# Router logits of an attention and mixture-of-experts kernel: from x and the attention output as nine more columns of Wo, instead of from the normed rows

## What is computed

```python
x1 = x + attention(layernorm(x), ctx)            # 16 heads of 16; ends with  out @ Wo + bo
xn2 = layernorm(x1)
logits = xn2 @ Wr                                # 8 experts
w, experts = top_2(softmax(logits)), softmax of the two
y = x1 + sum over the two experts of  w * (silu(xn2 @ gate) * (xn2 @ up)) @ down
```

## Time and profile before

| | before |
|---|---|
| median of 3 runs | 1244.41 us |
| the profiled execution, its own time | 1243.54 us |
| its span, first to last instruction | 1241.8 us |
| busy: PE, DVE, ACT, POOL | 97%, 52%, 45%, 34% |
| granted TensorE clock, mean | 0.996 |
| moved by DMA | 112.43 MB |

### The profile page before, as it was taken

How to read it: one execution, slowest core, us unless ns; L and a number is a source line. 1 busy time by engine, 2 the same in 40 slices (tenths; PEclk the granted TensorE clock), 3 DMA queues, 4 the chain that set the end, 5 groups by cost and what they waited for, 6 DMA issues and landing times.

```text
span 1241.8 us, 30499 instructions
## 1 busy us (share of the span) xinstructions
PE 1209.8 (97%) x11102; PEld 989.2 (80%) x11103; DVE 645.0 (52%) x1744; ACT 562.3 (45%) x926; POOL 425.4 (34%) x356
## 2 busy tenths in 40 slices
PE   7999999999999999899999999999999999999996
PEld 5777777777667766688888888888888888888995
DVE  3778888888788878834462222222222222222332
ACT  4566666666666666535422222222222222222542
POOL 4112333333333333253454422222222222222322
PEclk9999999999999999999999999999999999999998
DMA  5444455455455432434444433333333333333432
GB/s 148 135 118 126 148 155 151 149 159 154 151 154 153 123 117 88 101 86 62 75 78 80 70 51 52 51 51 51 51 51 51 51 51 51 52 51 41 54 51 31
DMA packets 171585, 112.43 MB, mean 91 GB/s; under 512 B 103344, under 2 KB 158640, under 8 KB 171472
## 3 DMA queue, kind: packets, MB, share of 16 engines
q1 hardware_dynamic: 143984, 72.75, 24.0%
q0 software_dynamic: 26400, 37.09, 17.3%
q10 hardware_dynamic: 1088, 1.05, 0.2%
HBM read 48.59 MB, written 45.46 MB: 76 GB/s over the span
## 4 chain that ended last, share of the span: by engine, by line
PE 93%; DVE 3%; DMA 2%; issue 1%; ACT 1%; SPq 0%; POOLq 0%; DVEq 0%
PE banks L545 73%; PE banks L574 5%; PE banks L588 5%; PE banks L599 5%; PE banks L580 1%; PE banks L551 1%; PE banks L615 1%; DMA heads<-qT 1%; PE banks L623 1%; DVE row_max L1088 1%; DMA out<-x_sb,token 1%; DMA ctxT_sb<-in_ctx 1%; DVE q_less L1095 0%; DVE att_rows L1101 0%; SPq L293 0%
## 5 line engine op out<-in xcount | busy, mean ns | idle before, releaser
L494 POOL DMA_INDIRECT out<-x_sb,token x135 | 210.6, 1560 | 418.9 <-DVE x_sb L1402 373.5
L919 ACT ACTIVATE qT<-banks 128x1024 f32<-128x1024 f32 (+1 forms) x75 | 70.4, 939 | 462.8 <-PE banks L545 441.5
L1396 DVE TENSOR_TENSOR heads<-qT,banks 128x1024 f32<-128x1024 f32 (+1 forms) x75 | 83.6, 1114 | 346.8 <-PE banks L545 339.0
L545 PE MATMUL banks<-down_sb,heads 128*128 x1080 | 245.5, 379 | 0.9 <-DVE heads L1396 0.9
L545 PE MATMUL banks<-xnT,kT 128*128 128x256 f32 (+1 forms) x1216 | 243.0, 357 | 0.0
L545 PE MATMUL banks<-xnT,probs 128*128 128x256 f32 (+1 forms) x1184 | 238.7, 359 | 0.0
L545 PEld LDWEIGHTS banks<-xnT,kT 128*128 128x128 f32 x1216 | 211.9, 190 | 25.5 <-issue 0.2
L545 PEld LDWEIGHTS banks<-xnT,probs 128*128 128x128 f32 x1184 | 208.3, 190 | 25.2 <-issue 0.2
L545 PEld LDWEIGHTS banks<-down_sb,heads 128*128 128x128 f32 x1080 | 204.0, 190 | 28.2 <-issue 1.1
L443 POOL DMA_INDIRECT sorted_x<-xn,slots_now x128 | 125.5, 980 | 275.2 <-PE banks L574 133.1
L1088 DVE TENSOR_REDUCE row_max<-banks 128x16 f32<-128x2048 f32 x64 | 146.6, 2291 | 51.0 <-PE banks L574 50.8
(11 more groups left out here) (172 smaller groups left out, 1272.0 us busy)
## 6 DMA issues: line engine op xcount, KB each, us to landing
xn<-sorted_x SPq DMA_DIRECT2D x240, 64.0 KB
x_sb<-in_x SPq DMA_DIRECT2D x16, 512.0 KB, 3.9
ctxT_sb<-in_ctx SPq DMA_DIRECT2D x16, 512.0 KB
heads<-kT SPq DMA_DIRECT2D x128, 64.0 KB
heads<-qT SPq DMA_DIRECT2D x128, 64.0 KB
out<-x SPq DMA_DIRECT2D x16, 512.0 KB
gate_sb<-_L_ffn_kernel_gating_EDF SPq DMA_DIRECT2D x8, 512.0 KB
up_sb<-in_L_ffn_kernel_up_EDF SPq DMA_DIRECT2D x8, 512.0 KB
```

The costliest lines, as they stand in the source:

```text
L494: pool.indirect_dma_start(out=out[:, :], out_offset=bass.IndirectOffsetOnAxis(ap=token[:, v, h:h + 1], axis=0), in_=ys[:, 2 * u + h, :], i ...
L545: last = nc.tensor.matmul(dst, lhsT, rhs, start=(i == 0), stop=(i == len(pairs) - 1))
L919: nc.scalar.activation(gatedT[:, 0:w * F], all_banks[:, 1024 * place:1024 * place + w * F], ACT.Silu).then_inc(s_silu, 1)
L1396: nc.vector.tensor_tensor(fusedT[:, u, 0:w * F], gatedT[:, 0:w * F], gate_up[:, 1024:1024 + w * F], ALU.mult).then_inc(s_fuse, 1)
```

## The change

The logits of a normed row are rstd * (x1 Wr - mean * colsum(Wr)). And x1 Wr = x Wr + attn (Wo Wr) + a constant. So:

- `wo_sb` gets 9 more columns: Wo Wr (8) and minus their sum, so that the sum over a row of 265 is still the sum over 256. `project` and `add_residual` work on 265 columns (`WIDE`); x1 and x_bo are as wide.
- The host hands over x transposed and Wo transposed as well. SP loads x's second layout once per group (512 KB) in b=1. `route_logits(g)` takes x Wr of the group itself from it in b=0, `swap_logits(g)` follows in b=1, and DVE adds the constants and writes them to x_bo's 9 columns (`keep_x_logits`).
- `x1_swapped` and `copy_x1T` are gone (8 transposes and 2 copies a group).
- DVE keeps the raw logits of a complete group in b=1 (`keep_raw`, two operations with both operands in SBUF), and multiplies by rstd one group later in `route_shift` (one operation more).
- At the start: Wo Wr and the constants are made on TensorE within sequences 0 and 1; four small DVE operations ahead of them.
- After stage A only `places` and the count are left on TensorE between the units.

```diff
+WIDE = D + EXPERTS + 1
...
+            def load_xT(g):
+                wait(sp, s_logitT, g)
+                sp.dma_start(xT_sb[:], xT[:, bass.ds(g * GROUP * TOK, GROUP * TOK)].rearrange("(c p) t -> p c t", p=P)).then_inc(s_xT, 16)
...
             spread_queries(1)
+            sp.dma_start(woT_sb, woT.rearrange("(c p) n -> p c n", p=P)).then_inc(s_woT, 16)
+            load_xT(0)
...
                     if b == 1 and g > 0:
                         store_x1(g - 1)
+                    if b == 1 and g + 1 < GROUPS:
+                        load_xT(g + 1)
...
-                product(bank[:, 0:D], [(attnT[:, c * P:(c + 1) * P], wo_sb[:, c, :]) for c in range(DC)]).then_inc(s_proj, 1)
-
-            def x1_swapped(g, c, bank):
...
+                product(bank[:, 0:WIDE], [(attnT[:, c * P:(c + 1) * P], wo_sb[:, c, :]) for c in range(DC)]).then_inc(s_proj, 1)
...
             def route_logits(g, bank):
 
-                wait(pe, s_n2Tc, g * 2 + 2)
+                wait(pe, s_xT, g * 16 + 16)
...
                         wait(pe, s_less, i * 2 + 2)
-                        if b == 1 and prev2:
-                            wait(pe, s_route, (g - 2) * ROUTE_STEPS + SHIFTED)
+                        if b == 1:
+                            wait(pe, s_x_logits, g + 1)
                         norm_swapped(g + 1, b, other_bank(i, 3))
-                    if b >= 2 and prev:
-                        wait(pe, s_less, i * 2 + 2)
-                        x1_swapped(g - 1, b - 2, other_bank(i, 3))
-                    if b == 0 and prev2:
+                    if i == 0:
+                        wo_through_router(other_bank(i, 0))
+                    if b == 0 and core:
                         wait(pe, s_turn, i)
...
+            def keep_x_logits(g, u, bank):
+                wait(dve, s_logit, g + 1)
+                nc.vector.tensor_tensor(x_bo[:, u, :, D:WIDE], bank[:, 0:GROUP * 32].rearrange("p (s e) -> p s e", e=32)[:, :, 0:EXPERTS + 1],
+                                        bias_logits.unsqueeze(1).broadcast_to([P, GROUP, EXPERTS + 1]), ALU.add).then_inc(s_x_logits, 1)
+
+            def keep_raw(g):
+                wait(dve, s_x1, g * GROUP + GROUP)
+                wait(dve, s_route, (g - 1) * ROUTE_STEPS + 1)
+                nc.vector.tensor_tensor(raw_mean[:], over_group(router_sums), over_experts(x1_sum[:]), ALU.mult).then_inc(s_raw, 1)
+                wait(dve, s_raw, g * 2 + 1)
+                nc.vector.scalar_tensor_tensor(raw[:], raw_mean[:], -1.0 / D, x1[:, :, D:D + EXPERTS], ALU.mult,
+                                               ALU.add).then_inc(s_raw, 1)
+
+            def route_shift(g):
                 steps = Steps(dve, s_route, g * ROUTE_STEPS)
...
+                steps.then(nc.vector.tensor_tensor(logits[:], raw[:], over_experts(rstd2[:]), ALU.mult))
+                steps.then(nc.vector.reduce_max(best[:], logits[:], AX.X))
+                steps.done(nc.vector.tensor_tensor(logits[:], logits[:], over_experts(best[:]), ALU.subtract))
```

More of the change, by code:

```diff
@@ L134, in moe_attention @@
         logitsT = sb("logitsT", [P, TOK])
+        raw, raw_mean = sb("raw", GE), sb("raw_mean", GE)
+        router_sum = sb("router_sum", [P, DC])
+        bo_col = sb("bo_col", [P, DC])
+        router_consts = sb("router_consts", [P, 2, EXPERTS + 1])
+        bias_logits, router_sums = router_consts[:, 0], router_consts[:, 1, 0:EXPERTS]
         chosen = sb("chosen", GE, bf16)
@@ L314, in _ @@
             sp.wait_ge(s_zero, 1)
[L315 to L318, removed]
+            sp.dma_start(wr_sb[:, :, 0:EXPERTS], router.rearrange("(c p) e -> p c e", p=P)).then_inc(s_wr, 16)
+            sp.dma_start(bo_col[:], bo.rearrange("(c p) -> p c", p=P), allow_slow_non_contiguous=True).then_inc(s_bo_col, 16)
             sp.wait_ge(s_rows, 2)
@@ L654, in stage_a @@
                     wait(pe, s_turn, i - 1)
-                    if b == 1 and prev2:
-                        wait(pe, s_logitTc, g - 1)
-                    if b == 2 and prev2:
-                        wait(pe, s_route, (g - 2) * ROUTE_STEPS + SHIFTED)
+                    if b == 1 and core:
+                        wait(pe, s_logitTc, g + 1)
+                    if i == 1:
+                        pe.wait_ge(s_wo_wide, 1)
+                    if b == 2 and core:
+                        wait(pe, s_x_logits, g + 1)
                     if b == 3 and prev2:
@@ L700, in stage_a @@
                         wait(pe, s_less, i * 2 + 2)
+                        wait(pe, s_x_logits, 1)
                         norm_swapped(1, 1, other_bank(i, 3))
@@ L741, in _ @@
             pe.wait_ge(s_bv_rep, 1)
-            product(work[:, 0, 0:D], [(bv_rep[:, c, :], wo_sb[:, c, :]) for c in range(DC)]).then_inc(s_bvo, 1)
+            product(work[:, 0, 0:D], [(bv_rep[:, c, :], wo_sb[:, c, 0:D]) for c in range(DC)]).then_inc(s_bvo, 1)
             pe.wait_ge(s_piece_c, 2)
@@ L1334, in stage_a @@
                         first_stats(g + 2, (2, 3))
+                    if b == 1 and core:
+                        wait(dve, s_logit, g + 1)
+                    if i == 1:
+                        dve.wait_ge(s_consts_r, 1)
+                        nc.vector.tensor_copy(router_consts[:], other_bank(i, 3)[:, 2 * P:2 * P + 32].rearrange(
+                            "p (k e) -> p k e", e=16)[:, :, 0:EXPERTS + 1]).then_inc(s_wo_wide, 1)
+                    take_max_off(i, other_bank(i, 3))
+                    if i == 0:
+                        dve.wait_ge(s_wo_wr, 1)
+                        nc.vector.tensor_copy(wo_sb[:, :, D:WIDE], other_bank(i, 0)[:, 0:32].rearrange(
+                            "p (c e) -> p c e", e=16)[:, :, 0:EXPERTS + 1]).then_inc(s_wo_wide, 1)
+                    if i == 1:
+                        dve.wait_ge(s_wo_wide, 2)
+                    if b == 1 and core:
+                        keep_x_logits(g, u, other_bank(i, 3)[:, P:2 * P])
                     if b == 1 and prev2:
-                        wait(dve, s_logit, g - 1)
-                    take_max_off(i, other_bank(i, 3))
-                    if b == 1 and prev2:
-                        route_shift(g - 2, other_bank(i, 3)[:, P:2 * P])
+                        route_shift(g - 2)
                     if b == 2 and prev2:
@@ L1365, in stage_a @@
                         route_first(g - 2)
+                    if b == 1 and prev:
+                        keep_raw(g - 1)
                     if b == 3 and g == EARLY_GROUPS + 2:
@@ L1416, in behind_tile @@
                 if t == 3:
+                    route_shift(GROUPS - 2)
+                    keep_raw(GROUPS - 1)
                     second_eps(GROUPS - 1)
-                if t == 5:
-                    route_shift(GROUPS - 2, att)
                 if t == 6:
@@ L1431, in behind_tile @@
                 if t == 12:
-                    route_shift(GROUPS - 1, att)
+                    route_shift(GROUPS - 1)
                     route_first(GROUPS - 1)
```

125 lines of the change are left out of this document (57 added, 68 removed).

## The result

| | before | after |
|---|---|---|
| median | 1244.49 us (4 runs, 1242.09 to 1245.66) | 1279.94 us (4 runs, 1274.21 to 1282.84) |
| ratio, 95% interval | | 1.0282 (1.0242 to 1.0321) |
| the profiled execution, its own time | 1243.54 us | 1280.81 us |
| its span | 1241.8 us | 1279.1 us |
| busy: PE, DVE, ACT, POOL | 97%, 52%, 45%, 34% | 94%, 53%, 43%, 33% |

The prediction was 1275 us (1250 to 1284), slower with a chance of 0.88.

What follows compares the result with a forecast made beforehand. The prediction saw PE nearly full, with a slackless DVE chain in b=1 and b=2. Terms 31.6 - 3.0 - 0.9 + 1.5 - 0.9 + 4.0 - 0.4 = +31.9 on 1243.54 gave 1275 us, range 1250 to 1284.

Steps and rivals of the forecast that it cites:

- The place and the mechanism: b=2: DVE's four added operations push its two-SBUF-input operations behind POOL's keep_x start in every group; chance 0.74.
- The lock's price: b=2: waiting for POOL costs 2.16 (shift held) to 2.78 (rest held) a group; 2.6 taken, 31.6 with group 10.
- the shift's mean above 1 us: Profile after: DVE's second_shift should average above 1 us, where it was 0.28, if held by POOL.
- rival A: b=2, groups 2 to 14: DVE late but not held by POOL; 0.67 a group, 8.7 in all, 1252 us; chance 0.12.
- Group 15: It has no keep_x: about +0.7 in b=2 against as much less in b=3, sum 0.
- b=3: Transposes gone before scores_swapped: at most 0.38 a group, the queries' DMA next in line; 0.3 in ten groups, -3.0.
- b=1: Norm transposes no longer wait for route_shift; next scores hangs on ACT: -0.07 a group, -0.9; nine more columns add 0.034.
- b=0: Nine more columns in project lengthen PE's path by 0.034 a step; three steps of 15 groups, +1.5 in all.
- The transposes' worth of nothing in b=2: Without its transposes PE waits for turn_att instead: worth 0 in groups 2 to 14, 0.4 once in group 1.
- Start: Sequences 0 and 1: DVE waits for Wo Wr, x of group 1 loads later, constants added; +4, between 1 and 8.
- Tail: Stage B, where PE is full: the last group's transposes gone, -0.9; moved x Wr matmuls counted as 0.
- B: PE is the bound after all: DVE's additions fit before scores of b=2 ends, so faster, 1233 us; chance 0.08.

Runs made afterwards that it cites:

- single wait: The changed kernel with one wait added: POOL's keep_x in b=2 also waits for DVE's second_shift; 1242.64 us, ratio 1.0016.
- six-operation version: The kernel before with six small idle DVE reduces added in b=1 behind route_first, none with two SBUF inputs; 1275.49 us, ratio 1.0254.
- after_again: The changed kernel itself, nothing altered, profiled again on the same chip as a repeat of the kernel before (1244.88 us); 1278.51 us.

## Why the prediction held, step by step

**The place and the mechanism: right.** DVE's additions pushed it past POOL's fixed start in b=2 of every group, PE waits for `row_max`, and that step alone lost 38.7 us, where the whole lost 37.3. Shown by the single wait (8.05 instead of 9.81 at equal times of DVE) and by the idle operations alone (+31 us).

**The lock's price: 2.6 taken, 2.83 measured** (10.49 - 7.66, the groups at the full clock); the upper end, 2.78, was right. `rest` rather than the shift was held in nine of the 13 groups, `raw` in three (3, 7 and 11), the shift in group 2 alone. Each time it was the first DVE operation with two SBUF inputs after POOL's start, and reduces passed. That is what the Trainium skill (SBUF — State Buffer, Who interferes with whom) says, and the traces agree: `rest` 2.36 us, and in the six-operation version the reduce `second`, inside POOL's span, 0.19. (The reduce that the prediction named, at 348.97, had begun 0.02 ahead of POOL.) The choice of 2.6 over 2.78 left room for a `rest` that slips ahead of POOL, and in this trace that happened in group 2 alone. In sum 33.9, which is the 38.7 less the 4.8 of the clock below, where 31.6 was predicted.

**The sign that was wrong:** the text gave "the shift's mean above 1 us" as the mark of the lock. It is 0.29. Once `rest` has waited for POOL, POOL is done when the shift comes. By that mark alone a reader would have decided for rival A, though the text's own upper end implied what happened.

**The clock: no term at all.** PE's new idle time of 2.5 to 2.6 us was followed by the lower clock in six of 12 groups, 0.80 each, 4.8 us. Group 15, taken at 0, lost 3.4: its clock fell to 0.90 and 0.82 (528 to 545 and 545 to 556 us), where its `scores_swapped` records lasted 2.09 us instead of 1.17 and 1.23. In the version with POOL's wait b=0 and b=1 of group 15 ran at 1.00 and took 7.83 and 7.33 instead of 9.14 and 7.63, so about 1.6 of the 3.4 are the clock there; in b=2 (+1.1) clock and DVE's order weren't separated.

**b=3:** -4.0 in sum, where -3.0 was forecast, but not as told. In the seven groups in which PE waits for nothing it takes 7.26 to 7.28, 0.45 below 7.72: the transposes were worth all of their 0.44, and the DMA did not stand right behind them. In five others (4, 8, 9, 10, 12) PE waits 0.5 to 1.2 us for the queries' DMA, where the kernel before did so in two, and three of them became 0.4 to 0.6 longer. That the sum is near is in part luck. **b=1** -1.57, with the wider columns in it, where -0.4 was forecast; **b=0** +0.44, as forecast. The transposes' worth of nothing in b=2 was measured (7.68 against 7.66).

**Start: +4 taken, +4.25 measured** at `scores` of group 2, with some luck: about 1.5 of it is the clock, which fell in sequence 1 of this trace (11.38 us at 0.85; 9.84 at 1.00 in after_again) and had no term. The parts that were told are there: statistics of group 1 1.8 us later, router products and constants 0.9 and 1.3:

```profile
25.80 1.39 DVE L1054 BATCH_NORM_STATS2 stats<-x_sb 128x6 f32<-128x256 f32 x4
24.71 0.95 PE L562 MATMUL banks<-wr_sb,xn 128*128 128x9 f32 x8
```

**Tail:** from the last `scores` of stage A to the end -3.9. The prediction had -0.9 for eight transposes. By the times from start to start of PE's records it was twelve, four of them in b=3 of group 15: 1.5 us. The x Wr products and their turning back of two groups, told as moved to the front at a sum of 0, were 1.4. The remaining 1.1 wasn't traced to a row.

**The sum:** 31.9 forecast, 37.3 measured. The lock is 2.3 above its term, the clock in b=2 4.8, group 15 3.4 and the start (with group 1) 0.6; the other steps of groups 2 to 14 are about 2.5 below theirs and the tail 3.0. So the forecast comes within 5 us partly because what the clock cost was offset by gains that were taken too small.

**Rivals.** A (late, no lock; 1252) had a false condition. Its price of 0.67 a group, 8.7 us, wasn't confirmed either: the single wait leaves 0.40 a group and +2.1 in all, but at the early times of its chip. B (1233) was false for this order; its number is near what PE could gain with DVE out of the way: it took moving `route_shift`, `route_first` and `turn_att`, and gave 1231.6 (with the start mended as well).

## What to carry to other kernels

Before work is added to an engine's chain, look not only at its length but at what starts at a fixed time beside it. On this kernel 0.6 us of work a group cost 2.2 to 2.8, because it moved an instruction of 4 to 32 values per row behind the start of a POOL addition of 1024. If an operation's duration in one odd group is ten times its usual one and ends with another engine's instruction, measure its margin in all the other groups. Then move the work to a step with slack rather than adding a wait: with the wait the kernel was 2 us above the one before, on a chip where DVE was early; the moves brought it to 1% below.

## What was not expected of the hardware

- **The granted clock fell behind idle stretches of only 2.5 to 2.6 us** within a stage that is otherwise full, to 0.53, in six of 12 groups (five of 12 in after_again), and cost 0.8 us each time. In the six-operation version PE was idle for 1.9 us, and the clock fell in four of 13 groups, at 1.4 us each.
- **A very small operation is held for nearly all of another's run:** the shift, 128x4, took 2.33 us in group 2 of the six-operation version; in group 15 of the changed kernel, where POOL is idle, it takes 0.16.
- **The same place can differ between chips.** From group 3 on, the q_less of b=1 came 4.4 to 4.5 us after `scores` in all four kernels profiled on one chip and 4.9 to 5.5 on the others, with PE's work ahead of it at equal times (in group 5 within 0.03 us); the kernel before took 1240.5 there and 1243.9 to 1244.5 elsewhere. An edge of 0.06 us is moved by more than its width by that. The cause stays open.
